# Regrouping the inverse's row blocks, the transposes and the down projection in TensorE's order, and making two weight products later

## The reference

```python
x = x + A(layernorm(x))                     # outer residual, attention block
x = x + F(layernorm(x))                     # outer residual, feed-forward block

# A(u): a delta block and an MLP, each with its own residual
xh  = layernorm(u) * dn_g + dn_b
q, k, v = split(xh @ gates_w + gates_b); lr = xh @ lr_w + lr_b
k   = k / norm(k)
K   = tril(k @ k.T, -1);  w = solve_triangular(K + I, v)
y   = (q @ k.T) @ (lr * w)
u   = u + y @ out_w + out_b
u   = u + relu((layernorm(u) * mn_g + mn_b) @ w1 + b1) @ w2 + b2

# F(u): SwiGLU with int32 weights scaled by 1/127
F(u) = (silu(u @ wg.T) * (u @ wu.T)) @ wd.T   # hidden width 768
```

## Time and profile before

| | |
|---|---|
| median of 3 runs | 1553.88 us |
| profiled execution | 1553.63 us, its span 1551.9 us |
| PE busy | 1533.4 us, 99% of the span |
| PEld busy | 1362.1 us, 88% |
| DVE busy | 1151.1 us, 74% |
| ACT busy | 856.0 us, 55% |
| POOL busy | 767.0 us, 49% |
| granted TensorE clock | 1.0 (mean 1.000) |
| DMA | 178.24 MB, mean 115 GB/s |

### The profile page before, as it was taken

How to read it: one execution, slowest core, us unless ns; L and a number is a source line. 1 busy time by engine, 2 the same in 40 slices (tenths; PEclk the granted TensorE clock), 3 DMA queues, 4 the chain that set the end, 5 groups by cost and what they waited for, 6 DMA issues and landing times.

```text
span 1551.9 us, 30623 instructions
## 1 busy us (share of the span) xinstructions
PE 1533.4 (99%) x10840; PEld 1362.1 (88%) x10840; DVE 1151.1 (74%) x3075; ACT 856.0 (55%) x1692; POOL 767.0 (49%) x886
## 2 busy tenths in 40 slices
PE   8999999899999999999999999999999999999998
PEld 7999998788888888888888888888888888888887
DVE  7777884578877777788777777887777777777774
ACT  6877775355555555555555555555555555555553
POOL 5456872245444454444444544444444444444442
PEclk9999999999999999999999999999999999999999
DMA  7999998212222322222222222222222222222200
GB/s 247 347 312 321 323 335 259 62 62 76 76 76 75 116 76 76 76 75 74 70 73 106 81 74 76 75 76 76 75 100 78 76 76 75 76 75 75 73 17 28
DMA packets 150169, 178.24 MB, mean 115 GB/s; under 512 B 78850, under 2 KB 132098, under 8 KB 141826
## 3 DMA queue, kind: packets, MB, share of 16 engines
q1 hardware_dynamic: 150018, 176.28, 34.4%
HBM read 98.64 MB, written 77.59 MB: 114 GB/s over the span
## 4 chain that ended last, share of the span: by engine, by line
PE 80%; DVE 2%; ACT 1%; issue 0%; POOL 0%; DVEq 0%; ACTq 0%
PE ps L175 34%; PE ps L1142 23%; PE ps L1152 12%; PE ps L1073 4%; PE ps L1045 4%; PE ps L1062 2%; PE ps L1051 1%; PE ps L258 0%; PE ps L1183 0%; DVE xh3T_lo L1542 0%; DVE xinv L1487 0%; DVE low L199 0%; PE ps L1169 0%; DVE bt_lo L1542 0%; POOL gl_lo L1743 0%
## 5 line engine op out<-in xcount | busy, mean ns | idle before, releaser
L1767 POOL TENSOR_TENSOR hl<-late,hh 128x512 fp32r<-128x512 f32 x128 | 166.4, 1300 | 209.8 <-ACT hh L1347 209.8
L1342 ACT ACTIVATE late<-ps 128x512 f32<-128x512 f32 x192 | 114.3, 595 | 171.0 <-PE ps L1142 171.0
L1537 DVE TENSOR_TENSOR late<-ps,late 128x512 f32<-128x512 f32 x192 | 132.7, 691 | 94.9 <-PE ps L1142 93.1
L1152 PE MATMUL ps<-wdT,hh 128*128 128x256 f32 x744 | 199.8, 304 | 0.0
L1152 PE MATMUL ps<-wdT,hl 128*128 128x256 f32 x744 | 182.7, 281 | 0.3 <-DVE hl L1542 0.3
L1347 ACT ACTIVATE hh<-late 128x512 fp32r<-128x512 f32 x192 | 120.8, 629 | 108.7 <-DVE late L1537 108.7
L1714 POOL TENSOR_TENSOR sc<-ls,mhalf 128x4 f32<-128x4 f32 x64 | 65.7, 1026 | 221.4 <-DVE ls L1504 221.4
L1142 PE MATMUL ps<-xh3T_hi,wgT 128*128 128x512 f32 x384 | 153.7, 400 | 1.1 <-DVE xh3T_lo L1542 1.1
L1142 PE MATMUL ps<-xh3T_lo,wuT 128*128 128x512 f32 x384 | 151.9, 395 | 0.0
L1142 PE MATMUL ps<-xh3T_lo,wgT 128*128 128x512 f32 x384 | 151.8, 395 | 0.0
L1142 PE MATMUL ps<-xh3T_hi,wuT 128*128 128x512 f32 x384 | 151.5, 395 | 0.0
(11 more groups left out here) (220 smaller groups left out, 4730.8 us busy)
## 6 DMA issues: line engine op xcount, KB each, us to landing
xhT_scratch<-xhTk SPq DMA_DIRECT2D x32, 1024.0 KB, 6.7
xhT<-xhT_scratch SPq DMA_DIRECT2D x32, 1024.0 KB, 6.4
gg_scratch<-late SPq DMA_DIRECT2D x32, 640.0 KB, 4.1
gg<-gg_scratch SPq DMA_DIRECT2D x32, 640.0 KB, 3.9
xk<-in_L_attn_x_dram SPq DMA_DIRECT2D x32, 512.0 KB, 5.5
xt<-in_L_attn_x_dram SPq DMA_DIRECT2D x32, 512.0 KB, 4.1
out_dram<-late SPq DMA_DIRECT2D x31, 512.0 KB, 2.9
low_scratch<-late SPq DMA_DIRECT2D x128, 16.0 KB, 2.9
```

The costliest lines, as they stand in the source:

```text
L1152: mm = pe.matmul(ps[:, (FG, FU)[j // 2], (j % 2) * C:(j % 2 + 1) * C], part[:, h, blk(j)], wdT[:, h, :], start=(h == 0 and part is hh), st ...
L1342: act.activation(sg[:, h % 2, :], ps[:, FG, :], ACT.Silu, scale=QUANT).then_inc(sg_ev[h], 1)
L1537: dve.tensor_tensor(hf[:, h % 2, :], ps[:, up_bank(h), :], sg[:, h % 2, :], ALU.mult).then_inc(hf_ev[h], 1)
L1767: pool.tensor_tensor(hl[:, h, :], hf[:, h % 2, :], hh[:, h, :].bitcast(F32), ALU.subtract).then_inc(hl_ev[h], 1)
```

## The change

In TensorE's order (steps 2 to 31) row block 1 comes ahead of x2's transposes and row block 2 right behind them. `pe_down(0)` runs only hidden blocks 0 to 3 at first; `pe_down(1)` opens in another bank, and blocks 4 and 5 of both follow in turns. DVE's order follows: mask first, `hl` of blocks 4 and 5 behind the copies of row block 1, with the halves of `xh2T_lo` between them. The first weight product is made in step 0 of the main stage, as is the second, in the place of the dummy matmuls `keep_busy`; their operands lie in the memory of `a0` and `xa`. POOL's program is the same but for one wait in step 0. Step 5 of the weights' preparation (the second product) goes as step 4 does in the diff, and two further calls of `keep_busy(2)` and `keep_busy(4)` in step 0 give way to `pe_factors` of the second product with 2 and 4 matmuls; the last hunk of DVE's order stands at the end of `dve_body`.

```diff
-            whole = ((w2f, w22, None, 0), (w1f, w12, w1_done, CB), (wqk, wqk2, qk_done, 1), (wvo, wvo2, vo_done, 1))
+            whole = ((w2f, w22, None, 0), (w1f, w12, w1_done, CB))
             PREP = 8
-            SPLIT_AT = 6
+            PREP_PS = 4
+            SPLIT_AT = 4
...
-                if q == 4:
-                    pe.wait_ge(tq_done, 2)
-                    for m in range(CB):
-                        for h in range(2):
-                            for k in range(CB):
-                                mm = pe.matmul(piece(2 * m + h), wvT[:, k, m * P:(m + 1) * P], wo[:, k, h * P:(h + 1) * P],
-                                               start=(k == 0), stop=(k == CB - 1))
-                    mm.then_inc(vo_ps, 1)
...
+                def pe_factors(pe, i, lhs, rhs, quarters, last=False):
+                    if i > 0:
+                        return
+                    for q in quarters:
+                        m, h = q // 2, q % 2
+                        for k in range(CB):
+                            mm = pe.matmul(ps[:, S0, q * P:(q + 1) * P], lhs[:, k, m * P:(m + 1) * P],
+                                           rhs[:, k, h * P:(h + 1) * P], start=(k == 0), stop=(k == CB - 1))
+                    if last:
+                        mm.then_inc(factor_ps, 1)
...
+                DOWN = ((A2, 0), (FG, 0), (FU, 0), (FU, C))
...
                     if down:
                         after(pe, sg_ev[HB - 1], i - 1)
-                        pe_down(pe, i, 0, range(HB - 1))
+                        after(pe, a0_ev[TB - 1], i)
+                        pe_down(pe, i, 0, range(HB - 2 if att else HB - 1))
+                    if att and down:
+                        pe_row_block(pe, i, 1)
...
                         pe_transposes(pe, (FO0, FO1), xn, t2_ps)
                     if att and down:
-                        pe_row_block(pe, i, 1)
-                    if down:
+                        pe_row_block(pe, i, 2)
+                        pe_down(pe, i, 1, range(HB - 2))
+                        for h in (HB - 2, HB - 1):
+                            pe_down(pe, i, 0, (h,))
+                            pe_down(pe, i, 1, (h,))
+                    if down and not att:
                         pe_down(pe, i, 0, (HB - 1,))
                         pe_down(pe, i, 1)
-                    if att and down:
-                        pe_row_block(pe, i, 2)
                     if att and not down:
                         pe_row_block(pe, i, 3)
                         pe_weights(pe, i, 3)
-                        if i == 0:
-                            keep_busy(pe, S0, 4)
+                        pe_factors(pe, i, wvT, wo, range(2))
...
                         pe_weights(pe, i, 4)
-                        if i == 0:
-                            keep_busy(pe, S0, 2)
+                        pe_factors(pe, i, wvT, wo, range(2, 4), last=True)
...
                         if i == 0:
-                            keep_busy(pe, S0, 2)
+                            pe.wait_ge(factor_done, 1)
+                        pe_factors(pe, i, wkT, wqT, range(1))
...
                         pe_wstep(pe, i, 1)
+                        after(pe, ot_ev[0], i - 1)
                         pe_bt(pe, i, 3)
...
+                def act_factors(act, i, dst, n):
+                    if i == 0:
+                        act.wait_ge(factor_ps, n)
+                        act.activation(flat(dst), ps[:, S0, :], ACT.Copy).then_inc(factor_hi, 1)
...
                     act_weights(act, i, (4,))
+                    if att:
+                        act_factors(act, i, wvo2[0], 1)
...
+                def dve_factors(dve, i, lo, hi, n):
+                    if i == 0:
+                        dve.wait_ge(factor_hi, n)
+                        dve.tensor_tensor(lo, bank3(S0), hi.bitcast(F32), ALU.subtract).then_inc(factor_done, 1)
...
+                    if att and down:
+                        masked(dve, i)
                     if mlp:
...
-                    if att and down:
-                        masked(dve, i)
-                    if down:
-                        dve_hl(dve, i - 1, HB - 1)
-                    if att:
-                        row_block(dve, i, 1 if down else 2)
-                    if mlp:
+                    if att:
+                        row_block(dve, i, 1 if down else 2)
+                    if down and att:
+                        dve_hl(dve, i - 1, HB - 2)
+                        dve_lo(dve, xh2T2[1], xh2T2[0], (FO0, FO1), t2_hi, t2_ev, i, (0,))
+                        dve_hl(dve, i - 1, HB - 1)
+                        dve_lo(dve, xh2T2[1], xh2T2[0], (FO0, FO1), t2_hi, t2_ev, i, (1,))
+                    elif down:
+                        dve_hl(dve, i - 1, HB - 1)
+                    if mlp and not (down and att):
                         dve_lo(dve, xh2T2[1], xh2T2[0], (FO0, FO1), t2_hi, t2_ev, i)
...
-                        dve_hl(dve, i, 4)
+                        if i == NS - 1 or not att:
+                            dve_hl(dve, i, 4)
...
+                        if i == 0:
+                            pool.wait_ge(factor_done, 1)
                         pool.tensor_tensor(xa[:, :, :], xt[:, :, :], b2_bc[:, :].unsqueeze(1).broadcast_to([P, TB, C]),
```

More of the change, by code:

```diff
@@ L116, in delta_block_kernel @@
         wvo2 = pair("wvo", [P, CB, C])
+        a0 = sb("a0", [P, TB, C])
+        xa = sb("xa", [P, TB, C])
+        wkT, wqT, wvT, wo = a0[:, 0:CB, :], a0[:, CB:2 * CB, :], xa[:, 0:CB, :], xa[:, CB:2 * CB, :]
         w12 = pair("w1", [P, CB, C])
@@ L280, in delta_block_kernel @@
             wlr = sb("wlr", [P, CB, 2], c=pre)
-            wkT = sb("wkT", [P, CB, C], c=pre)
             s2 = pair("s", [P, CB, C], c=pre)
@@ L730, in delta_block_kernel @@
             mcol = sb("mcol", [P, 3, CB], c=pre)
-            wo = sb("wo", [P, CB, C], c=pre)
             w1raw = sb("w1raw", [P, CB, C], c=pre)
@@ L734, in delta_block_kernel @@
             wscaled = sb("wscaled", [P, CB, QV], c=pre)
[L735 to L738, removed]
             w1f = sb("w1f", [P, CB, C], c=pre)
@@ L744, in delta_block_kernel @@
             w_shift_ps, w_shift_done, bqv_done = sem("w_shift_ps"), sem("w_shift_done"), sem("bqv_done")
-            tq_ps, tq_done, vo_ps, vo_done = sem("tq_ps"), sem("tq_done"), sem("vo_ps"), sem("vo_done")
-            qk_ps, qk_done = sem("qk_ps"), sem("qk_done")
+            tq_ps, tq_done = sem("tq_ps"), sem("tq_done")
             b1_ps, b1_sb, b1_done, w1_done, bo_done = sem("b1_ps"), sem("b1_sb"), sem("b1_done"), sem("w1_done"), sem("bo_done")
@@ L760, in delta_block_kernel @@
             pieces = ps[:, T0 + 1, :].rearrange("p (q c) -> p q c", c=P)
-            def four(t):
-                return t.rearrange("p (q c) -> p q c", c=P)
             def load_low(sp):
@@ L882, in prep_evicted @@
             def prep_evicted(pe, q):
-                if 0 <= q < SPLIT_AT:
-                    done, count = ((w_shift_done, 1), (b1_sb, 1), (tq_done, 1), (tq_done, 2), (vo_done, 1), (qk_done, 1))[q]
+                if 0 <= q < PREP_PS:
+                    done, count = ((w_shift_done, 1), (b1_sb, 1), (tq_done, 1), (tq_done, 2))[q]
                     pe.wait_ge(done, count)
             def prep_pe(pe, q):
-                if 0 <= q < SPLIT_AT:
+                if 0 <= q < PREP_PS:
                     pe.wait_ge(xhT_lo[1], q + PREP + 2)
@@ L966, in delta_block_kernel @@
             m22 = pair("m2", [P, CB, C], c=mc)
-            a0 = mb("a0", [P, TB, C])
             bs2, mv2, ls2, sc2 = mb("bs2", [P, TB, 6]), mb("mv2", [P, TB, 2]), mb("ls2", [P, 2, TB]), mb("sc2", [P, 2, TB])
@@ L971, in delta_block_kernel @@
             h12 = pair("h1", [P, CB, T], c=mc)
-            xa = mb("xa", [P, TB, C])
             xh3T2 = pair("xh3T", [P, CB, T], c=mc)
@@ L1007, in delta_block_kernel @@
             wt_ps, wt_ev = sem("wt_ps"), sem("wt_ev")
+            factor_ps, factor_hi, factor_done = sem("factor_ps"), sem("factor_hi"), sem("factor_done")
             FFN_STEPS = 3 * HB * CB // 4
@@ L1151, in pe_down @@
                                 pe.wait_ge(made[h], i - 1)
-                            mm = pe.matmul(ps[:, (FG, FU)[j // 2], (j % 2) * C:(j % 2 + 1) * C], part[:, h, blk(j)],
+                            bank, c0 = DOWN[j]
+                            mm = pe.matmul(ps[:, bank, c0:c0 + C], part[:, h, blk(j)],
                                            wdT[:, h, :], start=(h == 0 and part is hh),
@@ L1274, in pe_body @@
                         pe_weights(pe, i, 6)
-                        if i == 0:
-                            keep_busy(pe, S0, 2)
+                        pe_factors(pe, i, wkT, wqT, range(1, 2))
                     if down:
@@ L1298, in pe_body @@
                         pe_weights(pe, i, 8)
-                    if i == 0:
-                        keep_busy(pe, S0, 4)
+                        pe_factors(pe, i, wkT, wqT, range(2, 4), last=True)
                     if mlp:
```

(7 more changed lines are left out.)

## The result

The changed kernel takes 1570.60 us (median of 4 runs, 1568.04 to 1571.54), the kernel before 1553.91 us beside it: ratio 1.0102, 95% interval 1.0089 to 1.0115. It is slower, by 1.0%; the forecast was 1557.1 us, range 1549.0 to 1560.8. The profiled execution took 1571.06 us (span 1569.3), 17.43 us more than the one of before, where +3.2 had been summed.

What follows compares the result with a forecast made beforehand. TensorE (PE) was taken to bound the full steps, 39.30 us each. Terms -3.6 + 0.2 + 6.6 = +3.2 us took 1553.63 to 1556.8 us profiled, 1557.1 us as median; range 1549.0 to 1560.8.

Steps and rivals of the forecast that it cites:

- the loss of the full steps: Steps 2 to 31: later z step outweighs PE's gain, 0.22 us a step, +6.6 us, from +3.0 to +9.9.
- Part 1: Keys stage: two weight products leave it, PE saves 3.57 us, an ACT eviction costs 0.2; sum -3.4 us.
- Rival C: Keys stage gives nothing back since the DMAs pace it, the rest as forecast: 1560.7 us, slower; chance 0.08.
- Part 2: Full steps, PE alone: regrouped row blocks and down products gain 0 to 0.2 us a step, 0.1 taken.
- Part 3: Full steps, DVE and POOL: later `hl` 5 moves `xa2` onto `gl_hi`; z step 3 starts 0.19 us later.
- the hold: POOL's `xa2` holds up DVE's cast `gl_hi`, which ends at 1204.55 instead of 1203.83 in step 24.
- a longer z step: Third row block: a z step that waited lasts 0.70 us where this one lasts 0.59.
- what the second `h_lo` gives back: PE behind the z step: a matmul no longer waits for the second `h_lo`, so 0.08 us comes back.
- Step 24 stands for all 30: Full steps: they repeat each other closely, so step 24's timeline was used, its 0.22 us loss taken times 30.
- A: Full steps: POOL and DVE don't hold each other up; -6.4 us, 1547.5 us, faster; chance 0.15.
- B: Full steps: hold exists but the chain before the z step is 0.1 us shorter; about 1554 us, no change; chance 0.11.
- the seven links: Full steps: chain in front of the z step, summed from seven links, each length read from one row.

Runs made afterwards that it cites:

- e3: Changed kernel with POOL's `xa2` adding only 1 of 4 row blocks in steps 2 to 31; 1554.01 us, ratio 0.9996.
- e5: Kernel before with the regrouping alone, and `hl` of blocks 4 and 5 ahead of both `xh2T_lo` halves; 1549.74 us, ratio 0.9974.
- e6: Changed kernel with the cast `gl_hi` made on ACT instead of DVE; 1556.43 us, ratio 1.0015.
- e8: e2's kernel with the load of x's first block issued seven sequences earlier in the keys stage; 1549.71 us, ratio 0.9974.
- e2: Kernel before with only the two weight products moved to step 0 of the main stage; 1553.07 us, ratio 0.9989.
- e10: Changed kernel with `hl` of blocks 4 and 5 side by side and x's first block loaded seven sequences earlier; 1548.28 us, ratio 0.9960.

## Why the prediction was wrong

Its mechanism was right and its side too; two terms of the sum were mis-sized: the gain at the end of the keys stage (-3.4 us, measured +0.2) and the loss of the full steps (+6.6 us, measured +17.2).

- **Part 1, -3.4 us.** The sequences do take 7.31 to 7.36 and 3.58 us are saved up to the last one (3.57 forecast). The step that failed is "3.57 us go if nothing else comes up": the last Gram's copies waited for a store (+1.74) and step 0 ran at a low clock (+1.56); with the first transposes 0.55 later in this execution, step 2 starts 0.23 us later than before instead of 3.4 earlier. Rival C named the DMAs, but as a pace of the whole stage, which the sequences of 7.3 us contradict, and the clock stands nowhere. This is 3.6 of the 14.2 us by which the profiled time missed.
- **Part 2, 0 to 0.2 us a step for PE.** e3 says 0, as its lower bound; 0.22 once `hl` 5 comes earlier (e5), just over the upper one.
- **Part 3, the hold.** `hl` 4 came at 2.98 us after the step's start, as computed. Then four links were each a little short. The first half of `xh2T_lo` started 0.72 us behind `hl` 4 and not 0.60, so `hl` 5 came 0.13 late. Why is not shown: `hl` as such isn't it, since behind `hl` 5 the other half did start after 0.60, and in e5 the second `hl` 0.61 behind the first. `xa2` took 2.43 and not 2.40 (+0.03). The cast ended 0.42 after it, as taken. The copies started 0.03 behind its end and not 0.03 before (+0.06), and the z step 0.15 behind the copies and not 0.06 (+0.09). Together +0.3: the z step starts 0.50 later in the step, not 0.19. The remaining terms, a longer z step and what the second `h_lo` gives back, came within 0.03 of the forecast and cancel.
- **"Step 24 stands for all 30"** failed in steps 8 and 16. The memset behind `xa2` cost nothing before, since the cast then ran after both; now it lengthens the hold by its own 0.95 us. That is 1.44 and 1.38 in place of 0.5.

Steps 2 to 30, by this: 27 x 0.51 + 1.44 + 1.38 = 16.6 us, and 0.6 with step 31 and what follows, against 30 x 0.22 = 6.6. This is 10.6 of the 14.2 us.

Rivals A and B fell: the pair does collide, and the chain in front of the z step was longer than summed, not shorter. The range failed as its upper end kept the single step at 0.33, which lets nothing come back from `h_lo` and gives DVE no overlap, but has no room for errors of the seven links in series: 0.04 us too little at each of the seven is 0.3 a step and 8 us in all.

## What to carry to other kernels

When an operation on GpSimd is released by one on VectorE, moving the releaser moves the GpSimd operation, and what VectorE does between SBUF tiles in its new window may end only after it, as the cast and `h_lo` did here: write both engines' windows side by side for every kind of step, the rare ones too. A chain of many links that multiplies by the number of steps needs a bound per link. A gain at a stage's end is only real when what the next stage waits for (here a store's buffer, then the clock) comes earlier too.

## What the runs showed of the hardware

- The hold seems to go both ways. Beside DVE's `hl` (1197.51, 0.68 long), POOL's operation on `xn` took 1.09 us before; with only work of DVE beside it that takes an input from PSUM, it takes 0.56 in the changed kernel. No run moves this pair alone. POOL and DVE of before and POOL of after, step 24:

```profile
1197.45 1.09 POOL L1727 TENSOR_SCALAR work<-a,sc 128x256 f32<-128x256 f32 x1 [0.20 <-POOL sc L1723]
1197.51 0.68 DVE L1542 TENSOR_TENSOR hl<-late,hh 128x512 fp32r<-128x512 f32 x1
```

```profile
1210.71 0.56 POOL L1745 TENSOR_SCALAR work<-a,sc 128x256 f32<-128x256 f32 x1 [0.20 <-POOL sc L1741]
```

- The tail of a held-up DVE operation after POOL's end has a size by operation: 0.42 us for a cast of 768 elements, 0.55 for a two-input operation of 512, each close to the operation's own length less the 0.14 of start-up.
- The granted clock at the border was 0.58 in the 3.2 us after PE had idled 3.05 us, 0.50 after 2.11 us (e3) and 2.50 us (e6), and 1.00 after 1.29 us (e8) and 1.81 us (e2's profiled run). Step 0 took 31.9 to 32.0 us in the first three and 30.5 in the others. Idle time just before is not all of it: at the start of the keys stage e10's clock fell with PE busy for 3.44 of the 4.00 us from 5 to 9, while the changed kernel's stayed at 1.00 with 2.57.
- From DVE's last copy to a z step that waits for it lie 0.15 us (typical step of the changed kernel), where a z step waiting for another operation had shown 0.06.
